# A recurrent block with a mixture of experts: three weight tiles cut from 128 to the 16 or 17 rows and columns in use

## The chip, the core and the metric

The kernel runs on one core of a Trainium2 chip. The core has five engines with a queue each: TensorE (PE) multiplies, VectorE (DVE), ScalarE (ACT) and GpSimd (POOL) work on tiles, SyncE (SP) issues DMAs. They meet only at semaphores. The metric is the time of one execution on the device in microseconds; lower is better.

A product on PE is two instructions: LDWEIGHTS loads the stationary operand (the profile's PEld), MATMUL streams the moving one through it and writes PSUM. A product of two fp32 operands is split into two such pairs, one of fp32r operands is one pair.

## What is computed

The input x is (32, 256, 128): 32 sequences of 256 tokens with 128 features. Cut to what matters here:

```python
xn = layernorm(x) * ln_w + ln_b
u = xn @ Ws.T + bs + xn @ Wi.T + bi               # 16 states per token
def step(h, u_t):
    h = tanh(h @ A.T + u_t)                       # 256 steps, 32 sequences at once
H = scan(step, 0, u)
out = H @ Wo.T + bo
gate = sigmoid(xn @ Wg.T + bg)
x1 = layernorm(x + out * gate + x)
scores = softmax(x1 @ gate_w.T)                   # 8 experts, the best 2 by scores + gate_b
h_e = silu((x1 @ w1[e] + b1[e]) * (x1 @ w3[e] + b3[e]))    # 176 wide, all 8 experts
y = sum_e weight_e * (h_e @ w2[e] + b2[e]) + shared expert(x1)
result = layernorm(x1 + y)
```

## The kernel before

A tile is 16 time steps of all 32 sequences, 512 tokens; there are 16 tiles. Each engine runs the same function `one(k, ...)` for k from -3 to 16: the mixture of experts of tile k, the recurrence of tile k + 2 ("attn" and "norm" parts for tiles k + 1 and k + 2), the input norm of tile k + 3 and the output of tile k - 1. Every k is 13 positions of 3 slots. A position is one 128-wide block of the hidden layer (0 and 1 the shared expert, 2 to 12 the eight experts' 1408 columns); its main work on PE is three matmuls of w1 (L757 to L759), three of w3 (same lines), three of w2 for the position five back (L768 to L770, into `py`), and one that spreads the routing weights (L752, into the single buffer `prw`). ACT adds a bias (L403), DVE multiplies (L630), ACT takes silu (L382), DVE weighs with prw (L615), ACT and POOL split the product into a high and a low part (L392, L308). The smaller steps hang at fixed slots (tables `AT`, and `AT_START` for k below 0); nothing is scheduled at run time, each engine's order is the written one.

The lines that the change touches, all with fp32 operands:

- L705 at slot 10: `pu` <- `wsiT` and `xnT`, the 512 inputs u of the tile to come. `wsiT` holds (Ws + Wi) transposed in its first 16 columns and zeros in 112 more, so `pu` has 128 rows of which 16 are used. It waits for `v_ready`, that is for DVE to have read `pu` in L575 (x1).
- L716 from slot 11 to slot 38, 16 times per tile: one recurrence step, 32 columns of `pu` += `aT` times the last h. `aT` is 128x128 with A transposed in its corner and zeros elsewhere. ACT's L347 takes the tanh of rows 0 to 15 into `hT`, whose other rows are ones. h_ps and h_ready tie the two.
- L684 at slot 1: the output of the recurrence, `woT` times `hT`, 512 columns. `woT` has Wo transposed in rows 0 to 15, bo in row 16 (which meets the ones in `hT`) and zeros below.

DVE clears `vrow`, `woT`, `brow`, `aT`, `wsiT` and more at the start (L428 to L437). `rows_zeroed` follows `brow`, and SP and ACT wait for it before they load bo and small rows into those tiles.

Of the kernel before, what the change touches and what calls it, by code (L numbers as in the profile page):

```python
# [5 lines left out]
def rnn_gate_moe_block(nc, x, Ws, bs, Wi, bi, Wo, bo, Wg, bg, ln_w, ln_b, A,  # L6
# [4 lines left out]
    B, S, D = x.shape  # L11
    N = A.shape[0]
    E, _, H = w1.shape
    P = 128
# [27 lines left out]
    with ExitStack() as ctx:  # L42
        def sb(name, shape, dt=fp32):
            return ctx.enter_context(nc.sbuf_tensor(name, shape, dt))

        def pb(name, shape=(P, TOK)):
            return ctx.enter_context(nc.psum_tensor(name, list(shape), fp32))

        def sem(name):
            return ctx.enter_context(nc.semaphore(name))  # L50
# [11 lines left out]
        vrow, vcol = sb("vrow", [32, P]), sb("vcol", [P, 32])  # L62
        brow, bcol = sb("brow", [32, P]), sb("bcol", [P, 32])
        wg_t, gw_t, a_t = sb("wg_t", [D, D]), sb("gw_t", [E, D]), sb("a_t", [N, N])
        wsiT, woT, wgT, aT = sb("wsiT", [D, P]), sb("woT", [P, D]), sb("wgT", [D, D]), sb("aT", [P, P])
        gwT2 = sb("gwT2", [D, 2 * E], fp32r)
        bu, bgh = sb("bu", [N, 1]), sb("bgh", [D, 1])
        gb = sb("gb", [P, E])
# [13 lines left out]
        xnT = sb("xnT", [D, TOK])  # L82
        gth = [sb(f"gth{i}", [D, TOK]) for i in range(2)]
        hT = [sb(f"hT{i}", [P, TOK]) for i in range(2)]
# [33 lines left out]
        prw, py, pu, pm = pb("prw"), pb("py"), pb("pu"), pb("pm")  # L118

        vectors_loaded, biases_loaded, rows_zeroed = sem("vectors_loaded"), sem("biases_loaded"), sem("rows_zeroed")  # L120
# [4 lines left out]
        state_weights_ready, out_weights_ready = sem("state_weights_ready"), sem("out_weights_ready")  # L125
# [9 lines left out]
        ho_ps, og_ready, ogT_ps, v_ready = sem("ho_ps"), sem("og_ready"), sem("ogT_ps"), sem("v_ready")  # L135
# [15 lines left out]
        def iterations(eng, one):  # L151

            def straight(k):
                one(k, k % 2, k // 2, 0 <= k < TILES, 0 <= k + 1 < TILES, 0 <= k + 2 < TILES, k + 3 < TILES, 0 <= k - 1)
            for k in range(-3, 3):
                straight(k)
            with eng.Fori(0, (TILES - 6) // 2) as j:  # L160
                one(2 * j + 3, 1, j + 1, True, True, True, True, True)
                one(2 * j + 4, 0, j + 2, True, True, True, True, True)
            for k in range(TILES - 3, TILES + 1):
                straight(k)
# [28 lines left out]
        def out_bank(k):  # L193

            return py if isinstance(k, int) and k < 0 else pu
# [11 lines left out]
        def gated(slot, k, norm):  # L207
            return early(slot, k, norm, "gate")
# [12 lines left out]
        @block.sync  # L221
        def _(sp):
            def row(v):
                return v.rearrange("(a d) -> a d", a=1)

            sp.dma_start(xt[0][:, :, :].rearrange("p q d -> p (q d)"), xv[0]).then_inc(x_loaded[0], 16)
            for dst, src in ((ws_t, Ws), (wi_t, Wi), (a_t, A), (wg_t, Wg)):
                sp.dma_start(dst[:, :], src).then_inc(state_weights_loaded, 16)
            sp.dma_start(xt[1][:, :, :].rearrange("p q d -> p (q d)"), xv[1]).then_inc(x_loaded[1], 16)
            sp.wait_ge(rows_zeroed, 1)  # L230
            for dst, src in ((wo_t[:, :], Wo), (gw_t[:, :], gate_w), (woT[N:N + 1, :], row(bo))):
                sp.dma_start(dst, src).then_inc(out_weights_loaded, 16)
            sp.dma_start(w1f[:, 0:CH * P].rearrange("d (e h) -> d e h", e=E), w1.rearrange("e d h -> d e h")).then_inc(up_weights_loaded, 16)
            sp.dma_start(w1f[:, CH * P:HID + REST], sw1).then_inc(up_weights_loaded, 16)
            sp.dma_start(w3f[:, CH * P:HID], sw3[:, 0:P]).then_inc(up_weights_loaded, 16)
            sp.dma_start(w1f[:, HID + 64:HID + M13], sw3[:, P:H]).then_inc(up_weights_loaded, 16)
            for r, at, src, ssrc in ((0, 0, b1, sb1), (POS, 64, b3, sb3)):
                sp.dma_start(brow[r + 2:r + POS, :], src.rearrange("e h -> (e h)").rearrange("(c p) -> c p", p=P)).then_inc(biases_loaded, 16)
                sp.dma_start(brow[r:r + 1, :], row(ssrc[0:P])).then_inc(biases_loaded, 16)
                sp.dma_start(brow[r + 1:r + 2, at:at + REST], row(ssrc[P:H])).then_inc(biases_loaded, 16)  # L240
            sp.dma_start(gb[:, :], gate_b.partition_broadcast(P)).then_inc(gate_b_loaded, 16)

            sp.dma_start(w2t[:, 2:POS, :], w2.rearrange("e h d -> (e h) d").rearrange("(c p) d -> p c d", p=P)).then_inc(w2_loaded, 16)
            sp.dma_start(w2t[:, 0, :], sw2[0:P, :]).then_inc(w2_loaded, 16)
            sp.wait_ge(w2_zeroed, 1)
            sp.dma_start(w2t[0:REST, 1, :], sw2[P:H, :]).then_inc(w2_loaded, 16)
            for at in (64, 96):
                sp.dma_start(w2t[at:at + E, 1, :], b2).then_inc(w2_loaded, 16)
                sp.dma_start(w2t[at + E:at + E + 1, 1, :], row(sb2)).then_inc(w2_loaded, 16)

            def one(k, par, half, moe, attn, norm, pre, fin):
                if attn and (not isinstance(k, int) or k + 3 < TILES):
                    sp.wait_ge(v_ready, k + 2)
                    sp.dma_start(xt[1 - par][:, :, :].rearrange("p q d -> p (q d)"),
                                 xv[bass.ds(k + 3, 1)].rearrange("a b t f -> (a b) t f") if not isinstance(k, int) else xv[k + 3]
                                 ).then_inc(x_loaded[1 - par], 16)
                if fin:
                    sp.wait_ge(yo_ready, k)
                    sp.dma_start(ov[bass.ds(k - 1, 1)].rearrange("a b t f -> (a b) t f") if not isinstance(k, int) else ov[k - 1],
                                 yo[:, :, :].rearrange("p q d -> p (q d)")).then_inc(out_stored, 16)  # L260
            iterations(sp, one)
            sp.wait_ge(out_stored, 16 * TILES)
# [156 lines left out]
        def _(v):  # L419
            n = [0]  # L420

            def link(ins):

                n[0] += 1
                ins.then_inc(setup_dve, 1)
                v.wait_ge(setup_dve, n[0])

            nc.vector.memset(vrow[:, :], 0.0)  # L428
            nc.vector.memset(woT[:, :], 0.0)
            nc.vector.memset(brow[:, :], 0.0).then_inc(rows_zeroed, 1)  # L430
            nc.vector.memset(aT[:, :], 0.0)
            nc.vector.memset(wsiT[:, :], 0.0)
            nc.vector.memset(w2t[:, 1, :], 0.0).then_inc(w2_zeroed, 1)
            nc.vector.memset(w1f[:, HID + REST:HID + 64], 0.0)
            nc.vector.memset(hT[0][:, :], 1.0)
# [7 lines left out]
            def state_weights():  # L443

                v.wait_ge(setup_tr, 1)
                t = p1[0]
                link(nc.vector.tensor_copy(vcol[:, :], t[:, 320:352]))
                nc.vector.tensor_tensor(out=bu[:, :], in0=bsc, in1=bic, op=ALU.add)
                nc.vector.tensor_scalar(out=bgh[:, :], in0=bgc, scalar1=0.5, scalar2=None, op0=ALU.mult)
                nc.vector.tensor_copy(wsiT[:, 0:N], t[:, 0:N])  # L450
                nc.vector.tensor_copy(wgT[:, :], t[:, 144:144 + D])
                nc.vector.tensor_copy(aT[0:N, 0:N], t[0:N, 272:272 + N]).then_inc(state_weights_ready, 1)

            def out_weights():

# [193 lines left out]
        def _(pe):  # L649
            pe.wait_ge(id_made, 1)  # L650
            pe.wait_ge(setup_dve, 3)
            t = p1[0]
# [20 lines left out]
            def side(slot, k, par, half, moe, attn, norm, pre, fin):  # L673
# [7 lines left out]
                    four_transposes(pm, lambda q: xn[:, q, :], xnT_ps)  # L681
                if slot == AT['ho'] and attn:
                    pe.wait_ge(h_ready, STEPS * (k + 2))
                    nc.tensor.matmul(out_bank(k)[:, :], woT[:, :], hT[1 - par][:, :], start=True, stop=True).then_inc(ho_ps, 1)  # L684
                tile = gated(slot, k, norm)
                if tile is not None:
                    pe.wait_ge(xnT_ready, tile + 1)
# [13 lines left out]
                if slot == at('u', k) and norm:  # L701
                    pe.wait_ge(xnT_ready, k + 3)
                    if moe:
                        pe.wait_ge(v_ready, k + 2)
                    nc.tensor.matmul(pu[:, :], wsiT[:, :], xnT[:, :], start=True, stop=True, skip_group_check=True)  # L705
                if isinstance(k, int) and k == -2 and slot == 3:
                    out_weights()
                if isinstance(k, int) and k == -1 and slot == 0:
# [2 lines left out]
                t = chain_step(slot, k)  # L711
                if norm and t is not None:
                    c = step_cols(t)
                    before = hT[par if t else 1 - par][:, step_cols((t - 1) % STEPS)]
                    wait(pe, h_ready, STEPS * (k + 2) + t)
                    nc.tensor.matmul(pu[:, c], aT[:, :], before, start=False, stop=True,  # L716
                                     skip_group_check=True).then_inc(h_ps, 1)
                if slot == at('x1T', k) and attn:
                    pe.wait_ge(x1_ready, k + 2)
# [5 lines left out]
                if slot == at('logits', k) and attn:  # L725
                    pe.wait_ge(x1l_ready, k + 2)
                    wait(pe, v2_ready, k)
                    for q in range(Q):
# [4 lines left out]
                                               skip_group_check=True)  # L733
# [89 lines left out]
```

## Time and profile before

| | us |
|---|---|
| median of 3 runs | 687.93 (687.83 to 688.71) |
| the profiled execution, its own time | 688.71 |
| its span, first to last instruction | 687.0 |
| PE busy (matmuls) | 645.4 |
| PE busy (weight loads, beside the matmuls) | 510.5 |
| DVE busy | 525.5 |
| ACT busy | 479.2 |
| POOL busy | 436.4 |

The span has a start (to about 53 us) in which weights are prepared and the recurrence of two tiles runs without other work, a middle in which a round of 39.3 us repeats, and an end from 602 us on without recurrence. Engines overlap, so their times don't add up. Matmuls are pipelined: a record lasts longer than the engine is held, so the distance from one matmul's start to the next tells more than a duration.

In the rows below a shape such as 128*16 is the rows and columns of the array that an instruction uses.

### The profile page before, as it was taken

How to read it: one execution, taken by the hardware profiler on the slowest of the kernel's cores; microseconds unless marked ns; L12 is line 12 of the kernel's file. 1: busy time of each engine (PE TensorE's matmuls, PEld its weight loads, DVE VectorE, ACT ScalarE, POOL GpSimd, SP SyncE). 2: the span in 40 equal slices, each digit the busy share in tenths (PEclk: the TensorE clock that was granted, in tenths of full speed). 3: DMA queues.
4: the chain of work that ended last, by engine and by line, in shares of the span. 5: the costliest groups of instructions: out<-in, count | busy, mean ns of one | idle time of the engine just before them, and what ended most of it. 6: DMA issues, size and time to landing. Idle time of an engine off the chain costs nothing. (4 is left out here: it accounts for less than half of the span.)

```text
span 687.0 us, 11627 instructions
## 1 busy us (share of the span) xinstructions
PE 645.4 (94%) x3063; PEld 510.5 (74%) x3063; DVE 525.5 (76%) x1582; ACT 479.2 (70%) x978; POOL 436.4 (64%) x389
## 2 busy tenths in 40 slices
PE   4779999999999999999999999999999999999894
PEld 2556878778787877878787877878787787877672
DVE  6636768697887879688787869788787968788673
ACT  2325777777777777687777777777777768777672
POOL 5125675858576675857667585857667584767653
PEclk9999999999999999999999999999999999999998
DMA  6000000000000000000000000000000000000000
GB/s 179 0 16 16 2 0 16 17 15 17 17 0 30 3 15 15 15 15 15 15 0 15 15 15 15 15 15 0 24 7 15 15 17 1 16 1 16 1 8 23
DMA packets 9425, 11.28 MB, mean 16 GB/s; under 512 B 1198, under 2 KB 5300, under 8 KB 9396
## 3 DMA queue, kind: packets, MB, share of 16 engines
q1 hardware_dynamic: 8346, 10.23, 4.6%
q10 hardware_dynamic: 1050, 0.72, 0.4%
q8 instruction: 12, 0.20, 0.1%
q14 instruction: 17, 0.14, 0.1%
HBM read 6.75 MB, written 4.19 MB: 16 GB/s over the span
## 5 line engine op out<-in xcount | busy, mean ns | idle before, releaser
L308 POOL TENSOR_TENSOR low<-full,high 128x512 fp32r<-128x512 f32 x176 | 226.5, 1288 | 156.1 <-ACT high L392 156.0
L630 DVE SCALAR_TENSOR_TENSOR zt<-p,bcol,t 128x512 f32<-128x512 f32 (+1 forms) x208 | 154.8, 745 | 118.0 <-ACT t L403 105.7
L403 ACT ACTIVATE t<-p,bcol 128x512 f32<-128x512 f32 x192 | 132.2, 688 | 112.1 <-PE p L759 111.9
L716 PEld LDWEIGHTS pu<-hT,aT 128*128 128x128 f32 x512 | 101.2, 205 | 34.7 <-ACT hT L347 14.4
L615 DVE TENSOR_TENSOR full<-prw,sl 128x512 f32<-128x512 f32 x176 | 119.5, 679 | 6.9 <-ACT sl L382 2.6
L347 ACT ACTIVATE hT<-pu,bu 16x32 f32<-16x32 f32 x256 | 76.9, 301 | 57.7 <-PE pu L716 50.1
L382 ACT ACTIVATE sl<-zt 128x512 f32<-128x512 f32 x176 | 109.2, 621 | 0.4
L392 ACT ACTIVATE high<-full 128x512 fp32r<-128x512 f32 x176 | 108.5, 616 | 1.1 <-DVE full L615 1.0
L322 POOL TENSOR_TENSOR ex_ex<-napier,ex_ls 128x8 f32<-128x8 f32 x64 | 104.6, 1644 | 7.0 <-DVE ex_ls L522 7.0
L716 PE MATMUL pu<-hT,aT 128*128 128x32 f32 x512 | 89.4, 265 | 10.0 <-ACT hT L347 10.0
L757 PE MATMUL p<-x1h,w1l 128*128 128x512 f32 (+1 forms) x208 | 97.9, 471 | 0.1
L757 PE MATMUL p<-x1h,w3l 128*128 128x512 f32 x192 | 86.5, 451 | 0.0
L768 PE MATMUL py<-low,w2h 128*128 128x512 f32 x176 | 83.8, 476 | 0.8 <-POOL low L308 0.8
L759 PE MATMUL p<-x1h,w1h 128*128 128x512 f32 (+1 forms) x208 | 82.6, 397 | 0.0
L758 PE MATMUL p<-x1l,w1h 128*128 128x512 f32 (+1 forms) x208 | 82.3, 396 | 0.0
L759 PE MATMUL p<-x1h,w3h 128*128 128x512 f32 x192 | 76.1, 397 | 0.0
L758 PE MATMUL p<-x1l,w3h 128*128 128x512 f32 x192 | 76.0, 396 | 0.0
L752 PE MATMUL prw<-rwT,sel 128*128 128x512 f32 x176 | 70.7, 402 | 3.2 <-DVE full L615 1.6
L769 PE MATMUL py<-high,w2l 128*128 128x512 f32 x176 | 69.5, 395 | 0.0
L770 PE MATMUL py<-high,w2h 128*128 128x512 f32 x176 | 69.1, 393 | 0.0
L308 POOL TENSOR_TENSOR low_sh<-full_sh,high_sh 128x512 fp32r<-128x512 f32 (+1 forms) x32 | 42.3, 1320 | 27.6 <-ACT high_sh L392 27.6
L759 PEld LDWEIGHTS p<-x1h,w1h 128*128 128x128 f32 (+1 forms) x208 | 39.3, 189 | 9.4
(152 smaller groups left out, 1090.7 us busy)
## 6 DMA issues: line engine op xcount, KB each, us to landing
xt<-in_L_attn_x SPq DMA_DIRECT2D x16, 256.0 KB, 3.1
out<-yo SPq DMA_DIRECT2D x16, 256.0 KB, 2.5
w3f<-in_L_ffn_w ACTq DMA_DIRECT2D x1, 704.0 KB, 4.5
w1f<-in_L_ffn_w SPq DMA_DIRECT2D x1, 704.0 KB, 4.8
w2t<-in_L_ffn_w SPq DMA_DIRECT2D x1, 704.0 KB
w1f<-in_L_ffn_sw SPq DMA_DIRECT2D x1, 88.0 KB, 4.6
wg_t<-in_L_attn_Wg SPq DMA_DIRECT2D x1, 64.0 KB, 2.2
w3f<-in_L_ffn_sw SPq DMA_DIRECT2D x1, 64.0 KB, 4.2
```

Of the source, the lines that this page charges most:

```text
L308: g.tensor_tensor(out=lo[0:R, :], in0=full_of(pos)[0:R, :], in1=hi[0:R, :].bitcast(fp32), op=ALU.subtract).then_inc(low_ready, 1)
L322: g.tensor_tensor(out=ex8["ex"][:, q, :], in0=napier[:, q, :], in1=ex8["ls"][:, q, :], op=ALU.pow).then_inc(ex_ready, 1)
L382: nc.scalar.activation(sl[pos % 2][:, :], zt[(par + pos) % 2][:, :], ACT.Silu).then_inc(sl_ready, 1)
L392: nc.scalar.activation(parts_of(pos)[0][0:R, :], full_of(pos)[0:R, :], ACT.Identity).then_inc(high_ready, 1)
L403: nc.scalar.activation(t3[(par + pos) % 2][:, :], p3[(par + pos) % 2][:, :], ACT.Identity, bias=b3c[:, pos:pos + 1]).then_inc(t3_ready, 1)
L615: nc.vector.tensor_tensor(out=full_of(pos)[:, :], in0=prw[:, :], in1=sl[pos % 2][:, :], op=ALU.mult).then_inc(s_ready, 1)
L630: nc.vector.scalar_tensor_tensor(out=zt[(par + pos) % 2][0:R, :], in0=p1[(par + pos) % 2][0:R, :], scalar=b1c[0:R, pos:pos + 1], in1=t3[(p ...
L716: nc.tensor.matmul(pu[:, c], aT[:, :], before, start=False, stop=True, skip_group_check=True).then_inc(h_ps, 1)
L757: nc.tensor.matmul(o, wl, x1h[par][:, :], start=True, stop=False)
L758: nc.tensor.matmul(o, wh, x1l[par][:, :], start=False, stop=False)
L759: ins = nc.tensor.matmul(o, wh, x1h[par][:, :], start=False, stop=True)
L768: nc.tensor.matmul(py[:, :], w2h[:, pos, :], lo[:, :], start=(pos == 0), stop=False)
```

## The change

`wsiT` becomes 128x16, `aT` 128x16 and `woT` 17x128. The products use them whole: L705 and L716 write only rows 0 to 15 of `pu`, and L684 reads only 17 rows of `hT`. The two memsets of `woT` and `wsiT` go (every element is written now); that of `aT` stays, for its rows below 16. SP's wait for `rows_zeroed` moves behind seven DMAs, to just ahead of the first one into `brow`. Two lines fewer stand in the program, so what was L705, L716, L684 and L757 is L703, L714, L682 and L755.

```diff
-        wsiT, woT, wgT, aT = sb("wsiT", [D, P]), sb("woT", [P, D]), sb("wgT", [D, D]), sb("aT", [P, P])
+        wsiT, woT, wgT, aT = sb("wsiT", [D, N]), sb("woT", [N + 1, D]), sb("wgT", [D, D]), sb("aT", [P, N])
...
-            sp.wait_ge(rows_zeroed, 1)
             for dst, src in ((wo_t[:, :], Wo), (gw_t[:, :], gate_w), (woT[N:N + 1, :], row(bo))):
...
+            sp.wait_ge(rows_zeroed, 1)
             for r, at, src, ssrc in ((0, 0, b1, sb1), (POS, 64, b3, sb3)):
...
             nc.vector.memset(vrow[:, :], 0.0)
-            nc.vector.memset(woT[:, :], 0.0)
             nc.vector.memset(brow[:, :], 0.0).then_inc(rows_zeroed, 1)
             nc.vector.memset(aT[:, :], 0.0)
-            nc.vector.memset(wsiT[:, :], 0.0)
...
-                nc.vector.tensor_copy(aT[0:N, 0:N], t[0:N, 272:272 + N]).then_inc(state_weights_ready, 1)
+                nc.vector.tensor_copy(aT[0:N, :], t[0:N, 272:272 + N]).then_inc(state_weights_ready, 1)
...
-                    nc.tensor.matmul(out_bank(k)[:, :], woT[:, :], hT[1 - par][:, :], start=True, stop=True).then_inc(ho_ps, 1)
+                    nc.tensor.matmul(out_bank(k)[:, :], woT[:, :], hT[1 - par][0:N + 1, :], start=True, stop=True).then_inc(ho_ps, 1)
...
-                    nc.tensor.matmul(pu[:, :], wsiT[:, :], xnT[:, :], start=True, stop=True, skip_group_check=True)
+                    nc.tensor.matmul(pu[0:N, :], wsiT[:, :], xnT[:, :], start=True, stop=True, skip_group_check=True)
...
-                    nc.tensor.matmul(pu[:, c], aT[:, :], before, start=False, stop=True,
+                    nc.tensor.matmul(pu[0:N, c], aT[:, :], before, start=False, stop=True,
```

On PE no instruction changes its place. Around slots 10 to 12 of a round its queue reads, before (a row is a product: output, stationary and moving operand, and the rows and columns of the output):

```order
L705 MATMUL pu<-xnT,wsiT 128x512
L768 MATMUL py<-low,w2h 128x512
L769 MATMUL py<-high,w2l 128x512
L770 MATMUL py<-high,w2h 128x512
L752 MATMUL prw<-rwT,sel 128x512
L716 MATMUL pu<-hT,aT 128x32
L757 MATMUL p_1<-x1h,w1l 128x512
```

and in the changed kernel:

```order
L703 MATMUL pu<-xnT,wsiT 16x512
L766 MATMUL py<-low,w2h 128x512
L767 MATMUL py<-high,w2l 128x512
L768 MATMUL py<-high,w2h 128x512
L750 MATMUL prw<-rwT,sel 128x512
L714 MATMUL pu<-hT,aT 16x32
L755 MATMUL p_1<-x1h,w1l 128x512
```

The products with 16 rows of output stand between ones with 128. SP's queue near the start, before and then after, with the semaphore that an instruction waits for:

```order
L229 DMA xt<-in_L_attn_x 128x1x512
L232 DMA wo_t<-in_L_attn_Wo 128x16 [waits rows_zeroed]
L232 DMA gw_t<-in_L_ffn_gate_w 8x128
L232 DMA woT<-in_L_attn_bo 1x128
L233 DMA w1f<-in_L_ffn_w 128x8x176
L234 DMA w1f<-in_L_ffn_sw 128x176
L235 DMA w3f<-in_L_ffn_sw 128x128
L236 DMA w1f<-in_L_ffn_sw 128x48
L238 DMA brow<-in_L_ffn_b 11x128
```

```order
L229 DMA xt<-in_L_attn_x 128x1x512
L231 DMA wo_t<-in_L_attn_Wo 128x16
L231 DMA gw_t<-in_L_ffn_gate_w 8x128
L231 DMA woT<-in_L_attn_bo 1x128
L232 DMA w1f<-in_L_ffn_w 128x8x176
L233 DMA w1f<-in_L_ffn_sw 128x176
L234 DMA w3f<-in_L_ffn_sw 128x128
L235 DMA w1f<-in_L_ffn_sw 128x48
L238 DMA brow<-in_L_ffn_b 11x128 [waits rows_zeroed]
```

The DMAs keep their order; only the wait has moved, past seven of them.

## Rows read from the trace of the kernel before

**Rows 1.** The page's busy times: us, share of the span, instructions
```profile
PE 645.4 (94%) x3063; PEld 510.5 (74%) x3063; DVE 525.5 (76%) x1582; ACT 479.2 (70%) x978; POOL 436.4 (64%) x389
```

**Rows 2.** One stretch: length, busy us of PE, PEld, DVE, ACT, POOL, granted clock, DMA
```profile
220.83:260.09 39.26, 38.57 (x192) 31.03 (x192) 31.93 (x98) 29.66 (x62) 26.61 (x23) 1.00 0.04 14
```

**Rows 3.** Waits of PE, 60 to 602 us: total us, times, longest
```profile
PE pu L705 <- DVE x L575: 9.4, 14, 0.7
```

**Rows 4.** Timeline at one step: start, us, engine, line, array used, operands, count
```profile
201.35 0.31 PE L716 MATMUL pu<-hT,aT 128*128 128x32 f32 x2
...
201.40 0.27 PE L716 MATMUL pu<-hT,aT 128*128 128x32 f32 x1
...
201.81 0.39 PE L758 MATMUL p<-x1l,w1h 128*128 128x512 f32 x1
202.04 0.40 PE L759 MATMUL p<-x1h,w1h 128*128 128x512 f32 x1
...
201.46 0.19 PEld L757 LDWEIGHTS p<-x1h,w1l 128*128 128x128 f32 x1
201.57 0.19 PEld L758 LDWEIGHTS p<-x1l,w1h 128*128 128x128 f32 x1
```

**Rows 5.** Weight loads grouped by form: busy us, mean ns of one, idle before
```profile
L757 PEld LDWEIGHTS p<-x1h,w1l 128*128 128x128 f32 x192 | 36.8, 192 | 6.9 <-issue 3.4 <-DVE zt L630 0.5
...
L757 PEld LDWEIGHTS p<-x1h,w1l 128*112 128x112 f32 x16 | 2.8, 177 | 0.1
```

**Rows 6.** Timeline of the start, before 53 us: PE, weight loads, DVE
```profile
21.05 0.64 PE L716 MATMUL pu<-hT,aT 128*128 128x32 f32 x2 [0.40 <-ACT hT L347]
22.08 0.64 PE L716 MATMUL pu<-hT,aT 128*128 128x32 f32 x2 [0.40 <-ACT hT L347]
...
47.66 0.33 PEld L731 LDWEIGHTS pm<-gwT,x1h 128*128 128x128 f32 x1
47.87 0.33 PEld L732 LDWEIGHTS pm<-gwT,x1l 128*128 128x128 f32 x1
...
25.70 1.89 DVE L475 TENSOR_TENSOR w2l<-w2t,w2h 128x1664 fp32r<-128x1664 f32 x1
```

**Rows 7.** Timeline of the setup: weight loads, then PE
```profile
5.99 0.18 PEld L654 LDWEIGHTS p<-ident,wg_t 128*128 128x128 f32 x1
6.40 0.09 PEld L655 LDWEIGHTS p<-ident,a_t 16*16 16x16 f32 x1 [0.22 <-issue]
6.41 0.18 PEld L657 LDWEIGHTS p<-ident,vrow 32*128 32x128 f32 x1
...
11.17 0.14 PEld L661 LDWEIGHTS p<-ident,wo_t 128*16 128x16 f32 x1 [0.52 <-issue]
12.37 0.18 PEld L662 LDWEIGHTS p<-ident,gw_t 8*128 8x128 f32 x1 [1.06 <-issue]
...
11.17 1.06 PE L705 MATMUL pu<-xnT,wsiT 128*128 128x512 f32 x1
12.02 0.42 PE L661 MATMUL p<-ident,wo_t 128*16 128x128 f32 x1
```

**Rows 8.** Timeline of PE at L705 in the middle
```profile
220.83 1.10 PE L705 MATMUL pu<-xnT,wsiT 128*128 128x512 f32 x2 [0.69 <-DVE x L575]
```

**Rows 9.** Timeline of PE at L684 in the middle
```profile
211.09 1.02 PE L684 MATMUL pu<-hT,woT 128*128 128x512 f32 x2
```

**Rows 10.** Timeline of the setup on DVE and in SP's queue
```profile
1.17 0.17 DVE L430 MEMSET brow<- 32x128 f32 x1
...
4.05 0.49 DVE L487 BATCH_NORM_STATS2 stats_in<-xt 128x6 f32<-128x128 f32 x2 [1.01 <-DMA xt<-in_L_attn_x]
...
4.24 0.59 SPq L232 DMA_DIRECT2D wo_t<-in_L_attn_Wo  x1
```

**Rows 11.** Timeline behind x1: DVE's read of prw, PE's next write
```profile
227.42 0.66 DVE L615 TENSOR_TENSOR full<-prw,sl 128x512 f32<-128x512 f32 x1
...
228.39 0.39 PE L752 MATMUL prw<-rwT,sel 128*128 128x512 f32 x1
```

## The prediction

> **What bounds the kernel now.** I read the totals per engine first, then a stretch of the middle, then what TensorE waits for, then its own queue. TensorE (PE) is busy 94% of the span, the next engine 76% [rows 1]. In one round of the loop (220.83 to 260.09, from one L705 to the next) it is busy 38.57 of 39.26 us [rows 2]. From 60 to 602 us its matmuls wait for 9.4 us on DVE's x1 (L575), 14 times 0.7, and for hardly anything else [rows 3]. So in the middle the bound is TensorE's own queue, and what leaves it leaves the time. Before 53 us it is different: there the recurrence runs as a ping-pong between PE (L716) and ACT (tanh, L347), each waiting for the other [rows 6].
>
> **What one recurrence step costs in the middle.** 512-column matmuls follow each other every 0.23 us (L758 to L759, 201.81 to 202.04) [rows 4]. L716 starts at 201.35 and L758 at 201.81: 0.46, of which 0.23 is the stream of L757 between them. So a step costs PE 0.23 us, though it streams only 2 x 32 columns. The rest is weight loads. The loads of L757 and L758 start 0.11 apart (201.46, 201.57) [rows 4], which is what 128 columns take. L716's first load lies under the long matmul ahead; its second and that of L757 have nothing long above them: 2 x 0.11 = 0.22. The program has 16 x 16 = 256 steps, 32 of them before 53 us, 224 in the middle.
>
> **Part 1, the recurrence with 16 columns (aT).** A load with 16 fewer columns is 0.015 us shorter (L757: 177 ns for 112 columns, 192 for 128) [rows 5], and one of 16x16 takes 0.09 where one of 128x128 takes 0.18 (L655, L654) [rows 7]: about 0.9 ns a column by both, so 112 columns fewer are 0.10 us and the second load of L716 all but vanishes. The load of L757 keeps its 128 columns but can't start before the second matmul of the pair has. That can be 0.05 after the first (201.40 and 201.35) [rows 4]. New cost: 0.05 + 0.11 = 0.16, gain 0.07 a step. Bounds: 0.10, the whole saving of a load, and 0.045, since L661's load of 128 rows and 16 columns is only that much shorter than L654's (0.14 to 0.18) [rows 7]; I stay nearer to the middle, because L661's load ran under another matmul, which lengthens the record of any load. **224 x 0.07 = 15.7 us off** (10.1 to 22.4). The tanh moves forward with its matmul, and the next step's first load stays hidden.
>
> **Part 2, the same before 53 us.** There a step comes every 1.03 us (21.05, 22.08): PE 0.64, then the tanh and two handovers; PE idles 0.40 for it [rows 6]. Both loads of L716 are on the path, since the first waits for the tanh. Loads there start 0.21 apart (47.66, 47.87), against 0.11 in the middle: the engine is at the lower of its two levels, 1.2 GHz [rows 6, 4]. Two loads of 0.21 become two of 0.03; the first matmul's 0.05 us of streaming comes out from under the second load: 0.36 - 0.05 = 0.3 us a step. The lower bound is 0.19, twice the 0.09 to 0.10 between L654 and L655. 26 of the 32 steps are such round trips; 6 have their first load already behind transposes or another matmul and gain 0.2: 26 x 0.3 + 6 x 0.2 = 9.0. Not all of it arrives: in the second chain the logits at 47.66 need x1h and x1l, which don't get earlier by as much (0.6 by my count of steps between), and I take off 0.9 for other such places. DVE's splitting of expert weights ends at 25.70 + 1.89 = 27.6 [rows 6]; the first chain, today until 31.4, would end at 26.9 and its L684 at 28.8, so the splits stay covered by 1.2 us. **7.5 us off** (5 to 9).
>
> **Part 3, wsiT with 16 columns (L705).** Its first load follows the wait for x1 (0.69 idle ahead of 220.83) [rows 8] and nothing hides it. It gets 0.09 shorter in 14 rounds: **1.3 us off** (0 to 1.5).
>
> **Part 4, woT with 17 rows (L684).** The streamed columns are the same, 2 matmuls of 512. But the array is now used as one 32-row block between uses of all rows, and the setup shows what that does [rows 7]. L655's load (16 rows) does not start beside L654's matmul but at 6.40, though L654's began at 5.99: its load 0.11, its 128 columns 0.21, and 0.09 beyond. Behind L661's matmul (12.02, all rows) L662's load (8 rows) comes at 12.37, 0.14 beyond the 0.21 it streams. So a change of the number of rows in use makes the next load wait until the array is empty: 0.08 to 0.14, plus the load of 0.11 that was hidden. Going in and coming out: 2 x (0.08 + 0.11) = 0.38 (0.30 if the 0.08 halves at the higher level; 0.50 with 0.14). It lies on the path, since L684 has no idle time ahead of it [rows 9]. **15 x 0.38 = 5.7 us on** (4.5 to 7.5).
>
> **Do changes in columns cost the same?** This decides the sign, as each step goes from 128 columns to 16 and back. Into it: L661 (128 rows, 16 columns) comes behind L705 (128x128). Its load starts at 11.17, together with L705's second matmul, and its matmul at 12.02, 0.85 later, the 2 x 512 passes of that matmul and no more [rows 7]. Nothing was emptied. Out of it: L655's load (16x16) is followed 0.01 us later by L657's (32 rows, 128 columns) [rows 7]: the block of rows stays, the columns change, no gap. So I take zero. The pair 128x16 to 128x128 itself has no row.
> The Trainium skill, "TensorEngine Tiling (Array Packing)", section "Tiling Modes", says that changing the tiling mode, and not only the tile, drains TensorE, and it counts 128x32 as another mode than 128x128. The rows bear that out for rows and speak against it for columns; by its word rival A or B holds.
>
> **Part 5, setup.** Two memsets of DVE go, 0.17 each; behind them DVE idles 1.01 until x is there at 4.05, so nothing comes of it. SP reaches L232 at 4.24, long after the memset of brow (1.17 + 0.17), so its wait, moved past seven DMAs, is already met in both places [rows 10]. Order and number of DMAs stay. ACT's first DMAs leave 0.14 earlier, and what needs them (L657, 6.41) stands right behind L655 without a wait [rows 7]. Zero; the cover is 2.9 us of SP's issuing.
>
> **Sum.** -15.7 - 7.5 - 1.3 + 5.7 = -18.8 us. The profiled execution took 688.71 (span 687.0 and 1.7 around it), the highest of three; their median is 687.93. Against the one 669.9, against the median 669.1: I say **669**. With every bound at its end: 22.4 + 9 + 1.5 - 4.5 = 28.4 off, 659.5; 10.1 + 5 + 0 - 7.5 = 7.6 off, 680.3.
>
> **Rivals.**
> A, **leaving the 16-column form empties the array** (slower). Then behind each step L757's load waits for the end of the pair and 0.08 more: 0.05 + 0.03 + 0.08 + 0.11 = 0.27 against 0.23 now, +0.04; with 0.14, +0.10. 224 x 0.04 = 9, L705's exit 14 x 0.19 = 2.7, L684 5.7, less 7.5 and 1.3: +8.6, **696.5** (to 710). It decides the sign once an exit costs 18.8 / 238 = 0.08 a time above the forecast. For it: no row shows this very pair. Against: rows 7. Chance 0.11.
> B, **entering empties it too**: another 0.08 + 0.02 a step, 224 x 0.10 = 22: **719**. Against it L661's hidden load. Chance 0.03.
> C, **DVE holds the pace behind x1.** L752 writes one buffer, which DVE's L615 must have read: L615 ends at 227.42 + 0.66 = 228.08, L752 starts at 228.39 [rows 11], 0.31 later. Five steps lie between L705 and there, 5 x 0.07 = 0.35, so the cover is just used up. If DVE doesn't follow, 0.3 to 0.6 of a round's 1.1 us come back: 14 x 0.45 = 6, **675**; 684 if all of it does. Chance 0.09.
> D, **the change doesn't do what it says**, because narrow weights load no faster here: the gains go, L684 stays: **693.6**. Against it rows 5 and 7. Chance 0.03.
> The forecast has 0.74.
>
> **How the numbers follow.** The likeliest case gives 669 with its own range 659.5 to 680.3; C reaches to 684. A, B and D (0.17) are left out, and a little at the ends: 659.5 to 684 holds about 8 in 10. The three runs of before lie within 0.13%; about 0.2% (1.4 us) can be told from no change. Faster: 0.74 + 0.09 = 0.83. Slower: A, B, D less a little, 0.15. Within: 0.02.
> By the Trainium skill, "TensorE: Matmul & The Clock Gate", section "LDWEIGHTS (loading the stationary operand)", a load takes its columns over 1.2 in ns whatever the clock, 107 against 13: the early steps would save 0.19 instead of 0.3, and the sum would be about 672. The rows at 47.66 show 0.21 for a load.
>
> **What would show it.** Right: L758 starts 0.39 us after L716 instead of 0.46; a round takes 39.3 - 1.1 - 0.1 + 0.4 = 38.5 us; early steps come every 0.7 us; the loads of L684 and of what follows it start only after the matmul ahead. Rival A: the load of L757 starts 0.15 us or more after L716. Rival C: PE waits for L615 or L630 in the middle. I am wrong altogether if a 17-row matmul costs far more than 0.5 us, or if the lower clock level lasts beyond some 50 us.

## The result and the profile after

The changed kernel takes 725.23 us (median of 4 runs, 724.84 to 725.59), the kernel before beside it 687.91 (687.83 to 688.71): 1.0535 times as long (95% interval 1.052 to 1.055), 37.3 us slower. The forecast was 669, the range 659.5 to 684: wrong in sign. The profiled execution took 723.14, its span is 721.4.

Busy times of the page, one stretch (one round, from one L703 to the next; columns as in [rows 2]) and what PE waits for from 60 to 640 us:

```profile
PE 679.6 (94%) x3063; PEld 446.4 (62%) x3063; DVE 526.7 (73%) x1580; ACT 482.4 (67%) x978; POOL 438.7 (61%) x389
```
```profile
224.56:267.08 42.52, 41.83 (x191) 27.48 (x192) 32.02 (x98) 29.94 (x62) 26.75 (x23) 1.00 0.04 13
```
```profile
PE pu L703 <- DVE x L573: 9.0, 13, 0.7
```

The weight loads are busy for 64 us less than in [rows 1], and PE for 34 us more with the same 3063 matmuls. DVE, ACT and POOL work as long as before, in the round too [rows 2]. A round takes 42.52 us instead of 39.26, the granted clock is 1.00 in both, and PE waits for nothing new [rows 3]. So what was added lies in TensorE's own queue, where no other engine is named.

Two views show the place. First the queue of weight loads, 60 to 640 us, by what they waited for (us in total, times, longest), in which "issue" is time without a visible cause; behind it the step's loads grouped by form, over the whole kernel (busy us, mean ns of one, idle before):

```profile
PEld pu L714 <- issue: 81.0, 222, 0.4
PEld pu L703 <- issue: 11.7, 13, 0.9
...
PEld pu L682 <- issue: 4.9, 14, 0.4
```
```profile
L714 PEld LDWEIGHTS pu<-hT,aT 128*16 128x16 f32 x512 | 28.9, 96 | 99.9 <-issue 85.6 <-ACT hT L347 14.2
```

222 of the steps in the middle now have a load that stands idle for 0.36 us before it starts. Then one such step on the timeline, matmuls first and then the loads (columns as in [rows 4]):

```profile
201.43 0.40 PE L757 MATMUL p<-x1h,w1h 128*128 128x512 f32 x1
201.75 0.28 PE L714 MATMUL pu<-hT,aT 128*16 128x32 f32 x2
...
201.79 0.24 PE L714 MATMUL pu<-hT,aT 128*16 128x32 f32 x1
201.96 0.50 PE L755 MATMUL p<-x1h,w3l 128*128 128x512 f32 x1
202.29 0.39 PE L756 MATMUL p<-x1l,w3h 128*128 128x512 f32 x1
...
201.75 0.11 PEld L714 LDWEIGHTS pu<-hT,aT 128*16 128x16 f32 x2 [0.37 <-issue]
201.96 0.19 PEld L755 LDWEIGHTS p<-x1h,w3l 128*128 128x128 f32 x1
```

L757's 512 columns are in by 201.43 + 0.23 = 201.66. The first load of the step does not lie under them, as it did before [rows 4]: it starts at 201.75, 0.09 later. The second product of the pair starts at 201.79 and streams for 0.03; the next load, of L755, starts at 201.96, 0.14 after that, and its 0.11 are uncovered too. (The 0.03: the two matmuls of L684, with 512 fp32 columns, start 0.42 apart in the kernel before, at 211.09 and 211.51; 32 columns are a sixteenth of that.) 0.09 + 0.04 + 0.03 + 0.14 + 0.11 = 0.41 us that a step holds PE, where it was 0.23 and 0.16 was forecast. The 180 steps of the middle that stand, like this one, between long products all show it: from the product ahead to the second one behind it is 0.86 to 0.87 us, where most had 0.69 before.

The same at L682, the product with 17 rows (matmuls, then loads), and ahead of it the place in the kernel before:

```profile
210.85 0.40 PE L759 MATMUL p<-x1h,w3h 128*128 128x512 f32 x1
...
212.18 0.40 PE L769 MATMUL py<-high,w2l 128*128 128x512 f32 x1
```
```profile
214.20 0.39 PE L757 MATMUL p<-x1h,w3h 128*128 128x512 f32 x1
214.52 1.12 PE L682 MATMUL pu<-hT,woT 17*128 17x512 f32 x2
...
215.91 0.40 PE L767 MATMUL py<-high,w2l 128*128 128x512 f32 x1
...
214.52 0.29 PEld L682 LDWEIGHTS pu<-hT,woT 17*128 17x128 f32 x2 [0.35 <-issue]
215.57 0.19 PEld L766 LDWEIGHTS py<-low,w2h 128*128 128x128 f32 x1 [0.76 <-POOL low L308]
```

From the product ahead to the second one behind it was 1.33 and is 1.71: 0.38 more. At the start the steps come every 0.69 us instead of 1.03 [rows 6], and the second product of the out weights leaves at 47.97 instead of 55.67:

```profile
25.41 0.29 PE L714 MATMUL pu<-hT,aT 128*16 128x32 f32 x2 [0.40 <-ACT hT L347]
26.10 0.29 PE L714 MATMUL pu<-hT,aT 128*16 128x32 f32 x2 [0.40 <-ACT hT L347]
...
47.97 1.20 PE L682 MATMUL pu<-hT,woT 17*128 17x512 f32 x2
```

### The profile page after: what moved, and what is told of

It reads as the page before. It is cut to its first block and busy times, and to the rows that moved or that the text cites. A ratio compares the mean times of both kernels' runs of the same rounds, so it can differ in the third digit from the quotient of the medians.

```text
span 721.4 us, 11625 instructions
## 1 busy us (share of the span) xinstructions
PE 679.6 (94%) x3063; PEld 446.4 (62%) x3063; DVE 526.7 (73%) x1580; ACT 482.4 (67%) x978; POOL 438.7 (61%) x389
## 5 line engine op out<-in xcount | busy, mean ns | idle before, releaser
L322 POOL TENSOR_TENSOR ex_ex<-napier,ex_ls 128x8 f32<-128x8 f32 x64 | 106.6, 1674 | 4.0 <-DVE ex_ls L520 4.0
L755 PE MATMUL p<-x1h,w1l 128*128 128x512 f32 (+1 forms) x208 | 98.9, 475 | 0.1
L714 PEld LDWEIGHTS pu<-hT,aT 128*16 128x16 f32 x512 | 28.9, 96 | 99.9 <-issue 85.6
L755 PE MATMUL p<-x1h,w3l 128*128 128x512 f32 x192 | 87.1, 454 | 0.0
L757 PE MATMUL p<-x1h,w1h 128*128 128x512 f32 (+1 forms) x208 | 82.6, 397 | 0.0
L714 PE MATMUL pu<-hT,aT 128*16 128x32 f32 x512 | 71.4, 229 | 10.2 <-ACT hT L347 10.2
L766 PE MATMUL py<-low,w2h 128*128 128x512 f32 x176 | 75.8, 431 | 0.5 <-POOL low L308 0.5
L757 PE MATMUL p<-x1h,w3h 128*128 128x512 f32 x192 | 75.8, 395 | 0.0
L768 PE MATMUL py<-high,w2h 128*128 128x512 f32 x176 | 69.1, 392 | 0.0
L766 PEld LDWEIGHTS py<-low,w2h 128*128 128x128 f32 x176 | 32.9, 187 | 30.9 <-POOL low L308 12.3
```

The lines of the kernel that those rows point to most:

```text
L322: g.tensor_tensor(out=ex8["ex"][:, q, :], in0=napier[:, q, :], in1=ex8["ls"][:, q, :], op=ALU.pow).then_inc(ex_ready, 1)
L714: nc.tensor.matmul(pu[0:N, c], aT[:, :], before, start=False, stop=True, skip_group_check=True).then_inc(h_ps, 1)
L755: nc.tensor.matmul(o, wl, x1h[par][:, :], start=True, stop=False)
L757: ins = nc.tensor.matmul(o, wh, x1h[par][:, :], start=False, stop=True)
L766: nc.tensor.matmul(py[:, :], w2h[:, pos, :], lo[:, :], start=(pos == 0), stop=False)
```

## The experiments

The theory after the result, T in what follows: TensorE empties whenever the part of the array in use changes its form, columns as well as rows, and the forecast's evidence against columns was of another kind. The rivals: the narrow rows of `pu` or `aT` cost something by themselves, with any width under 128; or the 17-row product is what hurts; or L703's 16 columns are. All kernels here compute the whole reference, and each edit is against the kernel before, so lines keep their numbers except in hybrid, where they are four higher. Ratios are to the kernel before, run on the same chip beside them.

| kernel | us (lowest to highest) | before beside it | ratio (95%) | a round, us |
|---|---|---|---|---|
| before | 687.91 | | | 39.29 |
| changed | 725.23 (724.84 to 725.59) | 687.91 | 1.0535 (1.052 to 1.055) | 42.53 |
| a16 | 717.16 (715.79 to 717.49) | 685.96 | 1.0443 (1.0413 to 1.0473) | 42.02 |
| a64 | 727.32 (725.95 to 728.61) | 685.96 | 1.0599 (1.0565 to 1.0632) | 42.56 |
| a65 | 667.65 (666.83 to 668.09) | 685.96 | 0.9722 (0.9695 to 0.9748) | 38.42 |
| wo17 | 695.88 (694.88 to 696.02) | 685.96 | 1.0132 (1.0105 to 1.016) | 39.67 |
| plain661 | 688.13 (one run) | 687.42 | | 39.29 |
| aw16 | 718.30 (717.24 to 718.86) | 687.42 | 1.0448 (1.0418 to 1.0478) | 42.15 |
| aw65 | 667.34 (666.89 to 667.89) | 687.42 | 0.9711 (0.9684 to 0.9738) | 38.35 |
| hybrid | 665.98 (665.28 to 667.53) | 687.42 | 0.9689 (0.9662 to 0.9715) | 38.37 |
| a96 | 674.06 (673.73 to 674.11) | 686.33 | 0.9813 (0.9792 to 0.9835) | 38.67 |
| wo64 | 695.90 (one run) | 686.33 | | 39.68 |
| wo65 | 686.97 (one run) | 686.33 | | 39.27 |

### a16: the recurrence's weights alone

```diff
-        wsiT, woT, wgT, aT = sb("wsiT", [D, P]), ..., sb("aT", [P, P])
+        wsiT, woT, wgT, aT = sb("wsiT", [D, P]), ..., sb("aT", [P, N])
...
-                    nc.tensor.matmul(pu[:, c], aT[:, :], before, start=False, stop=True,
+                    nc.tensor.matmul(pu[0:N, c], aT[:, :], before, start=False, stop=True,
```

> Only aT is cut to 16 columns (and L716 writes 16 rows of pu); wsiT, woT and setup as before. Theory T, every switch between 128 and 16 columns empties the array: in the middle a step costs PE 0.40 us instead of 0.23 (the round of the changed kernel is 42.53 us against 39.29, of which L684 explains 0.38 and L705 0.12, which leaves 2.73 for 16 steps), rounds of 42.0 us, the start 7 to 8 us shorter: 718 us (715 to 721). Rival R1, it is the switch of rows at L684 that hurts and carries on into what follows: then this kernel is near the forecast without L684, 664 us.

717.16 us: this one edit is 31.2 of the 37.3. Its rounds are 2.73 us longer than before, 16 steps of 0.17. With the forecast's zero for columns it would have been faster than before.

### a64 and a65: on either side of half the array

```diff
+        ... sb("aT", [P, 64])
+                    nc.tensor.matmul(pu[0:64, c], aT[:, :], before, start=False, stop=True,
```

> Only aT is cut, to 64 columns (48 of them zeros). Theory T with the form decided by the columns in use, up to 64 being another form than 128: the array is emptied as with 16 columns, and both loads are longer than with 16 by 0.04 us, so a step costs 0.47 us: 687.9 + 224 x 0.24 - 4 in the start = 738 us (728 to 742). Rival R2, what hurts is only the very narrow load or the product with 16 rows of output, by degrees: then 64 columns lie between 16 and 128, some 700 us.

```diff
+        ... sb("aT", [P, 65])
+                    nc.tensor.matmul(pu[0:65, c], aT[:, :], before, start=False, stop=True,
```

> Only aT is cut, to 65 columns, one more than in a64. Theory T with the form changing at 64: no switch, the queue stays full, the second load of a step is 63 columns or 0.05 us shorter, 224 x 0.05 = 12 us less, and 2 x 0.1 us in each of 26 early steps, 5 us less: 671 us (666 to 677). Rival R2, by degrees: the same as a64 within 2 us.

One column parts 727.32 from 667.65. The step with 64 columns, matmuls and then loads:

```profile
202.43 0.40 PE L759 MATMUL p<-x1h,w3h 128*128 128x512 f32 x1
202.76 0.31 PE L716 MATMUL pu<-hT,aT 128*64 128x32 f32 x2
...
203.34 0.40 PE L769 MATMUL py<-high,w2l 128*128 128x512 f32 x1
...
202.76 0.19 PEld L716 LDWEIGHTS pu<-hT,aT 128*64 128x64 f32 x2 [0.36 <-issue]
203.00 0.19 PEld L768 LDWEIGHTS py<-low,w2h 128*128 128x128 f32 x1
```

and with 65:

```profile
212.09 0.40 PE L752 MATMUL prw<-rwT,sel 128*128 128x512 f32 x1
212.32 0.28 PE L716 MATMUL pu<-hT,aT 128*65 128x32 f32 x2
...
212.73 0.39 PE L758 MATMUL p<-x1l,w1h 128*128 128x512 f32 x1
...
212.09 0.37 PEld L716 LDWEIGHTS pu<-hT,aT 128*65 128x65 f32 x2
212.38 0.19 PEld L757 LDWEIGHTS p<-x1h,w1l 128*128 128x128 f32 x1
```

With 65 the first load starts at 212.09 together with the product ahead, under its stream, the wait "issue" is gone, and L758 comes 0.41 behind L716 (0.46 before [rows 4]). With 64 the load waits 0.36, until that product has streamed and 0.10 more. From the product ahead to the second behind it is 0.91 with 64 and 0.64 with 65. So neither the narrow `pu` nor narrow weights as such cost anything; the form 128x64 does, and 65 columns count as the whole array. The gain that Part 1 worked out is there as soon as the form stays: 0.87 us a round, 0.054 a step (the forecast's 0.07 was for 16 columns). With 64 the 727.32 lies just below the range that was named (728 to 742); it may be that the longer loads inside the pair are partly covered, but no run isolates it.

### wo17: the out weights alone

```diff
-                    nc.tensor.matmul(out_bank(k)[:, :], woT[:, :], hT[1 - par][:, :], start=True, ...
+                    nc.tensor.matmul(out_bank(k)[:, :], woT[0:N + 1, :], hT[1 - par][0:N + 1, :], start=True, ...
```

> Only L684 is cut, to 17 rows of woT and of hT; aT and wsiT keep 128 columns. Theory T: 0.38 us more in each of 15 rounds, as in the changed kernel, where the stretch from the matmul ahead of L684 to the second one behind it is 1.71 us against 1.32: 687.9 + 5.7 = 693.6 us (692 to 696). Rival R1: most of the 37 us, 715 or more.

A round is 0.38 longer, the forecast's figure. In span the profiled execution is 7.2 us over that of before (694.2 against 687.0); 14 rounds by 0.38 are 5.3. The rest is at the start. Five us there, wo17 and then before (length, busy us of PE with its number of matmuls, and so on, as in [rows 2]):

```profile
57.00:62.00 5.00, 5.00 (x12) 2.49 (x11) 2.68 (x10) 2.09 (x3) 0.41 (x1) 1.00 0.00 0
```
```profile
57.00:62.00 5.00, 4.82 (x21) 3.14 (x20) 3.73 (x24) 2.78 (x5) 0.15 (x1) 1.00 0.01 2
```

Long products follow each other there every 0.43 us in wo17, the pace of 1.2 GHz, until 61.9; in before they turn to 0.23 at 57.7. The clock of the two rows, 1.00, does not show it: in the profiles of wo65 and plain661 the granted clock reads 0.50 until 55.9 and 57.5, in these two it reads 1.00 throughout the start, and there the pace of the products has to be read. 4.2 us at half pace are 2.1 us lost. wo64 has the late rise too, at 61.8. Why it comes later there stays open; in the changed kernel the rise is at 48.2, in a16, a64, a65, aw16, aw65 and hybrid between 50.0 and 51.4.

The medians say more than the spans: wo17 is 9.9 us above the kernel before beside it (695.88 against 685.96). The rounds and the late rise make 7.4 of that; the other 2.5 can't be placed, as the kept profile of the kernel before was not taken beside it.

### plain661: the evidence of the forecast, with an ordinary product

L661 makes `wo_t` transposed, by the transpose instruction. The same matmul by the identity, as an ordinary product, does the same work.

```diff
-                nc.tensor.transpose(p1[1][0:N, 16:16 + D], wo_t[:, :], ident[:, :])
+                nc.tensor.matmul(p1[1][0:N, 16:16 + D], wo_t[:, :], ident[:, :], start=True, stop=True)
```

> The kernel before with one setup product in another form: Wo is transposed at L661 by an ordinary product with the identity instead of by a transpose instruction; 128 rows and 16 columns, right behind L705 (128x128), as before. Theory T2, rows 7 misled because fp32 transposes use all columns of the array whatever their shape: the ordinary product's first load no longer starts beside L705's second matmul (11.17) but about 0.1 us after its stream has ended, at 12.1 to 12.3 us. Rival: the load again starts beside it, and entering 16 columns is free when it happens once, so that something else empties the array in the recurrence. The time as a whole stays within 1 us of the kernel before.

The setup, PE and then its loads:

```profile
11.16 1.06 PE L705 MATMUL pu<-xnT,wsiT 128*128 128x512 f32 x1
...
12.15 0.13 PEld L661 LDWEIGHTS p<-ident,wo_t 128*16 128x16 f32 x2 [1.50 <-issue]
```

In [rows 7] the transpose's load starts at 11.17, beside L705's second product. Now it starts at 12.15: 0.85 for L705's stream, and 0.14 more. The view prints both alike, 128*16; they differ in the instruction alone. So a transpose of 16 columns did not change the form and an ordinary product does. The changed kernel holds the mirror image, a transpose behind a narrow product:

```profile
11.07 1.06 PE L703 MATMUL pu<-xnT,wsiT 128*16 128x512 f32 x1
...
12.06 0.09 PEld L659 LDWEIGHTS p<-ident,wo_t 128*16 128x16 f32 x1 [1.69 <-issue]
```

The same shape is printed for both, and yet the transpose's load waits for 0.85 and 0.14: leaving the narrow form for a transpose is a change. The Trainium skill, "TensorEngine Tiling (Array Packing)", "Tile-to-Partition Mapping", lists under its restrictions that column tiling rules out the transpose mode for fp32 inputs; the two traces agree, since these transposes behave as if they used the whole width.

### aw16 and aw65: the input weights too

```diff
-        wsiT, woT, wgT, aT = sb("wsiT", [D, P]), ..., sb("aT", [P, P])
+        wsiT, woT, wgT, aT = sb("wsiT", [D, N]), ..., sb("aT", [P, N])
...
-                    nc.tensor.matmul(pu[:, :], wsiT[:, :], xnT[:, :], start=True, stop=True, ...
+                    nc.tensor.matmul(pu[0:N, :], wsiT[:, :], xnT[:, :], start=True, stop=True, ...
```

(with the edit of a16; aw65 has 65 in all these places)

> aT and wsiT cut to 16 columns, woT whole: the changed kernel without its L684 edit. Theory T: over the kernel with aT alone (717.2) the exit of L705 costs 0.12 us in each of 14 rounds, 1.7 us: 718.9 us; and the changed kernel less this is L684's part, 6 us. Rival, edits that share a wait: within 0.5 us of 717.2.

> aT and wsiT cut to 65 columns, woT whole. Theory T: no switch; over the kernel with aT of 65 (667.7) L705's first load, which waits for x1, is 0.05 us shorter in 14 rounds: 0.7 us, 667.0 us. Rival: wsiT with fewer columns costs, as the wait for x1 takes it back or more: 667.7 or above.

With 16 columns L705 costs 0.13 a round more (42.15 against 42.02), with 65 it gives back 0.07 (38.35 against 38.42). Over 14 rounds these are 1.8 and 1.0 us; the medians, from different chips, can't tell so little. The changed kernel, which has L684's edit besides, is 0.38 a round and 6.9 us above aw16 (6 expected).

### hybrid: 16 columns at the start, 65 behind it

Before the loop, where `k` is negative, no long products stand between the steps.

```diff
+        def cut(k):
+            return N if isinstance(k, int) and k < 0 else 65
...
+                    nc.tensor.matmul(pu[0:cut(k), :], wsiT[:, 0:cut(k)], xnT[:, :], start=True, stop=True, ...
...
+                    nc.tensor.matmul(pu[0:cut(k), c], aT[:, 0:cut(k)], before, start=False, stop=True,
```

> As aw65, but for k below 0, where the recurrence of the first two tiles runs alone and PE waits for the tanh anyway, aT and wsiT are used with 16 columns. Theory T: there nothing is in the array to be waited for, and the two loads of a step shrink from 0.11 each (65 columns at 1.2 GHz) to 0.03, 26 x 0.1 to 0.16 = 2.6 to 4 us less: 663.5 us (661 to 666). Rival: each step's exit costs what its loads save: 667, as aw65.

665.98, the lowest of all, but only 1.4 below aw65, and the intervals overlap. The early steps do what was expected of them, 0.69 us instead of 0.82; aw65 first, then hybrid:

```profile
24.26 0.43 PE L716 MATMUL pu<-hT,aT 128*65 128x32 f32 x2 [0.40 <-ACT hT L347]
25.08 0.43 PE L716 MATMUL pu<-hT,aT 128*65 128x32 f32 x2 [0.40 <-ACT hT L347]
```
```profile
25.33 0.29 PE L720 MATMUL pu<-hT,aT 128*16 128x32 f32 x2 [0.40 <-ACT hT L351]
26.02 0.29 PE L720 MATMUL pu<-hT,aT 128*16 128x32 f32 x2 [0.40 <-ACT hT L351]
```

26 steps by 0.13 would be 3.4 us. What is missing goes in the start itself, at the six places where other products stand between two steps. One of them, hybrid and then aw65:

```profile
37.77 0.29 PE L720 MATMUL pu<-hT,aT 128*16 128x32 f32 x2 [0.40 <-ACT hT L351]
...
39.03 0.29 PE L720 MATMUL pu<-hT,aT 128*16 128x32 f32 x2
```
```profile
39.43 0.43 PE L716 MATMUL pu<-hT,aT 128*65 128x32 f32 x2 [0.40 <-ACT hT L347]
...
40.55 0.37 PE L716 MATMUL pu<-hT,aT 128*65 128x32 f32 x2
```

From step to step it is 1.26 with 16 columns and 1.12 with 65: there leaving and entering the narrow form costs more than the loads save, as the rival said of every step. The six are 0.13 to 0.31 longer, 1.1 us together; the longest of them, 5.62 against 5.31, holds L709 with its 16 columns (a16, whose input weights are whole, has 5.31 there). The other steps are some 3 us shorter together, and of the 1.9 that remain when the second product of the out weights starts (47.70 against 49.63), 1.4 are left at the last one (582.95 against 584.32), as much as the medians say.

Near its end the hybrid's profile has a stretch in which the granted clock is 0.50 (the eighth number of the row, after the busy times):

```profile
626.80:630.20 3.40, 3.00 (x7) 2.43 (x8) 0.69 (x1) 1.49 (x3) 1.28 (x1) 0.50 0.02 5
```

The kernel before has the same at 648.20 in its profile, the changed kernel none, and aw65 none before its last products. It may be why this execution took 667.53, 1.5 above the median; whether the others had it isn't known.

### a96: between 65 and 128

```diff
+        ... sb("aT", [P, 96])
+                    nc.tensor.matmul(pu[0:96, c], aT[:, :], before, start=False, stop=True,
```

> Only aT is cut, to 96 columns. Theory T: the form stays, and a step gets shorter by what one load of 32 columns less takes, 0.027 us, half of what 63 columns fewer gave (0.054): rounds of 38.86 us instead of 39.29, 224 x 0.027 = 6 us less, and some 3 us of the start: 677 us (674 to 681). Rival R3, the gain with 65 columns comes from something other than the load's length, such as fewer rows of pu written: then 96 columns give the same 667.7 or nothing at all.

Rounds of 38.67, 0.039 a step below before, where 65 columns give 0.054. So the gain goes with the columns, and rival R3 falls; but it isn't in proportion. The first 32 columns less give 0.039 and not the 0.027 that was expected (38.86 a round), the next 31 give 0.015, and the time is at the very edge of the range (674 to 681). Why is open. The loads of the step grouped by form, with 96, 65 and 64 columns:

```profile
L716 PEld LDWEIGHTS pu<-hT,aT 128*96 128x96 f32 x512 | 85.0, 172 | 40.6 <-ACT hT L347 14.3 <-issue 1.1
```
```profile
L716 PEld LDWEIGHTS pu<-hT,aT 128*65 128x65 f32 x512 | 70.7, 144 | 46.8 <-ACT hT L347 14.3 <-issue 1.2
```
```profile
L716 PEld LDWEIGHTS pu<-hT,aT 128*64 128x64 f32 x512 | 51.5, 142 | 98.6 <-issue 85.4 <-ACT hT L347 13.2
```

Above 64 the load gets shorter with its columns and "issue" stays at about 1 us. At 64 the load itself is no worse than at 65 (142 ns against 144), and 85.4 us of idle time appear.

### wo64 and wo65: the same limit in rows

```diff
+                    nc.tensor.matmul(out_bank(k)[:, :], woT[0:64, :], hT[1 - par][0:64, :], start=True, ...
```
```diff
+                    nc.tensor.matmul(out_bank(k)[:, :], woT[0:65, :], hT[1 - par][0:65, :], start=True, ...
```

> Only L684 is cut, to 64 rows. Theory T, the form decided at 64 for rows as for columns: the load of L684 starts about 0.1 us after the stream of the matmul ahead has ended, as with 17 rows; rounds of 39.66 us, 694 to 696 us. Rival: rows below 64 but above 32 lie between.

> Only L684 is cut, to 65 rows. Theory T: its load starts beside the matmul ahead, as with 128 rows; rounds of 39.3 us and the time of the kernel before within 1.5 us, as fewer rows make neither loads nor matmuls shorter.

With 64 rows (PE, then the load behind the product) it is as with 17:

```profile
213.70 0.40 PE L759 MATMUL p<-x1h,w3h 128*128 128x512 f32 x1
...
215.42 0.40 PE L769 MATMUL py<-high,w2l 128*128 128x512 f32 x1
...
214.03 0.29 PEld L684 LDWEIGHTS pu<-hT,woT 64*128 64x128 f32 x2 [0.36 <-issue]
```

With 65 it is as before:

```profile
209.23 0.40 PE L759 MATMUL p<-x1h,w3h 128*128 128x512 f32 x1
...
210.56 0.40 PE L769 MATMUL py<-high,w2l 128*128 128x512 f32 x1
```

1.72 and 1.33, against 1.71 in the changed kernel and 1.33 in that before; rounds 39.68 and 39.27. Rows bring no shorter load here, so 65 rows are worth nothing (686.97 beside 686.33).

## Why the prediction was wrong

**What failed.** One step, under "Do changes in columns cost the same?": "So I take zero." The measured figure is 0.09 going in and 0.14 coming out. (The uncovered load of 0.11 behind the pair was already in the forecast's 0.16.) Both pieces of evidence were transposes (L661, and the pair L655 and L657), and what the view prints as their columns is not what decides for them; plain661 shows that an ordinary product of L661's very shape waits. The text itself said that the pair 128x16 to 128x128 had no row. So the zero was an inference across kinds of instruction, on the one number that "decides the sign", and A and B, which it excluded, got a chance of 0.14 together.
The rule that it cited and set aside (the Trainium skill, "TensorEngine Tiling (Array Packing)", "Tiling Modes": changing the mode drains TensorE, and 128x32 is another mode than 128x128) is borne out for columns by a64 and a65: 0.91 against 0.64 us from the product ahead to the second behind.

**Part 1** took 15.7 us off by 0.16 a step. The step shown above holds PE for 0.41, and by a16's rounds the average one takes 0.17 more than before: 224 by 0.17 are 38 us on. The mechanism of shorter loads is right: with 65 columns it gives 0.054 a step for 63 columns, 0.86 ns a column, where the forecast took about 0.9 (a96 gives 1.2). In the changed kernel it is buried, since a load that begins only in an empty array has nothing to hide under.

**Part 2** came out in its number, in part by luck. Early steps take 0.69 (forecast 0.7), and the second L682 leaves 7.7 us earlier (forecast 7.5). But the six passings where other products stand between two steps, which were to give 1.2 us, give nothing (14.9 us together in both kernels), since in each the narrow form is left and entered again; and the 1.5 us that it took off for what would not arrive were not lost. The two errors nearly cancel.

**Part 3** had the wrong sign for the same reason: L703 to the second product behind it takes 1.28 (224.56 to 225.84) instead of 1.16 (220.83 to 221.99), 0.12 on in place of 0.09 off. The two rows of it, after and before:

```profile
225.84 0.39 PE L767 MATMUL py<-high,w2l 128*128 128x512 f32 x1
```
```profile
221.99 0.39 PE L769 MATMUL py<-high,w2l 128*128 128x512 f32 x1
```

**Part 4** was right to the digit, 0.38 a round. Its evidence in [rows 7] was of transposes too; in rows they do change the form, in columns they don't. **Part 5**, zero, is not tested by itself; the sum of the others closes without it.

**The sum, redone.** 38 + 14 x 0.12 + 15 x 0.38 - 7.7 = 37.8 us on; the medians say 37.3. The spans of the two profiles say 34.4. By the products of the out weights these are 6.1 us off up to the third (93.04 to 86.92), 42.0 on over the 13 rounds to the last (603.94 to 639.83 for it) and 1.5 off behind that, where the profile of before has its 3.4 us at half clock. The profiled execution of the changed kernel is also 2.1 us quicker than its median, for no reason that its trace shows.

**The rivals.** B is what happened, 719 against 725: it had 0.37 a step, with 0.08 coming out where 0.14 was measured, and otherwise the same steps. By the rounds a step takes 0.17 more and not B's 0.14, 224 x 0.03 = 7 us. It got a chance of 0.03. The sign named for leaving the form, the load behind the pair 0.15 us or more after the pair's start, is there: 0.21 (201.75 to 201.96). A falls: entering isn't free either (0.09 at 201.66). C does not show, not even where PE is really faster: with 65 columns (a65) PE waits, from 60 to 590 us, for

```profile
PE pu L705 <- DVE x L575: 9.0, 13, 0.7
```

and for L615 once, 0.2 us. That is no more than before. D is refuted by a65 and a96, whose loads take 144 and 172 ns on average against 205 with 128 columns.

## What to carry to other kernels

Between full-array matmuls, keep every small product on more than 64 rows and more than 64 columns of the array: 65 columns were worth 2.8% here, 16 or 64 cost 4.4% to 6.0%, and rows beyond 64 cost nothing. Cut further only where a narrow product stands alone in a ping-pong with another engine, as between most steps of the start here; hybrid had 1.4 us over aw65 by it, with intervals that overlap. All this was seen with fp32 products between fp32r ones of 512 columns; whether several narrow products in a row would share one change was not tried. And where a forecast's sign hangs on one zero, look whether the rows behind it are of the same kind of instruction as the one that changes; if none is, a rule that speaks against the zero deserves more than the 0.14 that it got here.

## What the runs showed of the hardware

- The form of the array in use is decided by the operand's size, with a limit between 64 and 65, in columns (727.32 against 667.65 us) and in rows (1.72 against 1.33 us around L684). No edit here asked for a form.
- Behind a change of form no load starts under the product ahead: it started 0.09 us after the last full-width column was in, and 0.14 after the last of a narrow product (0.13 with 64 columns: L768's load at 203.00). Behind the 17-row product it is 0.08: its second matmul starts at 215.06 and streams 0.43, the next load comes at 215.57. A recurrence step loses 0.23 by it, as much as the whole step held PE before.
- An fp32 transpose of 16 columns (L661) keeps the full form, although the trace prints 128*16 for it: its load starts at 11.17 beside the product ahead, that of an ordinary product of the same shape at 12.15.
- In a65, aw65, hybrid and a96 PE waited no more for other engines than before, though a round got up to 0.94 us shorter.
- The time at which PE reaches its higher level shifts from kernel to kernel by 14 us (48.2 to 61.9), and not only because the start gets shorter: behind the start of the second product of the out weights it comes after 0.2 us in the changed kernel, 2.0 in the kernel before and 5.8 in wo17. It moves the total by one or two us and makes single differences below 2 us hard to assign.
